# Turning the cross-attention's input on VectorE in 32x32 blocks instead of on TensorE

## What is computed

```python
x = _layernorm(x + attn(x, w_qkv, w_out))              # mixing: fft of q, k, v, cumulative sum of k*v, inverse fft
x = _layernorm(x + xattn(x, ctx, mask, W_q, b_q, ...)) # cross-attention, 16 heads of 32, 77 keys per batch
x = _layernorm(x + ffn(x, int4(kernel), bias, a, b))   # one 512x512 matmul with a rank-16 addition
```

## Time and profile before

| | |
|---|---|
| median of three runs | 940.3 us |
| the profiled execution | 941.81 us |
| span in it, first to last instruction | 939.4 us |
| TensorE busy | 885.9 us, 94% |
| VectorE busy | 669.9 us, 71% |
| ScalarE busy | 369.5 us, 39% |
| GpSimd busy | 373.9 us, 40% |
| mean granted TensorE clock | 0.975 of full speed |
| one loop step of `attend` | 58.0 us |

### The profile page before, as it was taken

The page is one execution under the profiler, slowest core; times in us unless marked ns, Lnnn a source line. Parts: engine busy times, 40 slices in busy tenths (PEclk is TensorE's granted clock), DMA queues, the critical chain, the costliest instruction groups (busy, mean ns, idle before and its releaser), DMA issues.

```text
span 939.4 us, 14604 instructions
## 1 busy us (share of the span) xinstructions
PE 885.9 (94%) x4284; PEld 733.5 (78%) x4284; DVE 669.9 (71%) x1132; ACT 369.5 (39%) x1403; POOL 373.9 (40%) x338
## 2 busy tenths in 40 slices
PE   5798999999999999999689999999999999999887
PEld 4683887888888888888578887888888888888675
DVE  3364467666666657567667978889788897988957
ACT  4152221212121111111487556665556655566611
POOL 2000364434353443315337544345343454434523
PEclk9897999999999999999789999999999999999999
DMA  6971710322314020104513140321403213030021
GB/s 184 283 203 48 177 45 34 102 66 70 95 39 134 22 68 23 67 24 143 180 23 101 30 136 11 97 67 32 132 11 94 67 44 119 12 93 19 18 79 45
DMA packets 85962, 76.02 MB, mean 81 GB/s; under 512 B 39895, under 2 KB 58583, under 8 KB 85919
## 3 DMA queue, kind: packets, MB, share of 16 engines
q1 hardware_dynamic: 85919, 75.49, 27.3%
HBM read 52.60 MB, written 22.87 MB: 80 GB/s over the span
## 4 chain that ended last, share of the span: by engine, by line
PE 37%; DVE 6%; ACT 5%; issue 2%; DVEq 0%; POOLq 0%; POOL 0%; ACTq 0%
PE shared_ps L130 28%; ACT probs L1410 4%; PE shared_ps L1204 3%; PE score_ps L130 3%; DVE score_ps L1715 2%; PE shared_ps L1166 1%; PE shared_ps L1237 1%; DVE top_s L1720 1%; ACT xT_hi L1423 1%; DVE xT_lo L1681 1%; DVE xT_lo L1673 1%; ACT qT_hi L1398 1%; DVE x_and_res L1761 0%; DVE pT_lo L1700 0%; DVE y L1739 0%
## 5 line engine op out<-in xcount | busy, mean ns | idle before, releaser
L1410 ACT ACTIVATE probs<-score_ps,top_s 128x77 f32<-128x77 f32 x512 | 158.8, 356 | 37.9 <-DVE top_s L1720 37.9
L1410 ACT ACTIVATION_READ_ACCUMULATOR probs<-score_ps,top_s 128x1 f32 x512 | 122.3, 239 | 0.0
L1559 POOL TENSOR_TENSOR probs<-probs,per_total 128x616 f32<-128x616 f32 x64 | 82.2, 1300 | 63.9 <-DVE per_total L1727 63.8
L1552 POOL TENSOR_TENSOR rstd<-ve,half_power 128x1 f32<-128x1 f32 x64 | 41.7, 652 | 153.4 <-DVE ve L1750 153.3
L1715 DVE COPY_PREDICATED score_ps<-hidden,masked 128x616 f32<-128x616 int32 x64 | 68.3, 1068 | 10.8 <-PE score_ps L130 10.5
L100 POOL TENSOR_TENSOR xT_lo<-x_tok,xT_hi 128x512 fp32r<-128x512 f32 x28 | 38.0, 1360 | 88.0 <-ACT xT_hi L96 88.0
L729 ACT ACTIVATE qT_hi<-vals 128x512 fp32r<-128x512 f32 x32 | 19.3, 628 | 119.1 <-POOL vals L776 103.8
L776 POOL TENSOR_TENSOR vals<-qs_prod 128x512 f32<-128x512 f32 x32 | 40.9, 1291 | 62.7 <-DVE qs_prod L862 62.7
L1417 ACT ACTIVATE pT_hi<-shared_ps 128x512 fp32r<-128x512 f32 (+1 forms) x96 | 47.7, 541 | 41.9 <-PE shared_ps L1204 41.6
L722 ACT ACTIVATE v_sb<-v_ps 128x512 f32<-128x512 f32 x32 | 18.9, 594 | 106.8 <-PE v_ps L130 106.8
L761 POOL TENSOR_TENSOR mix_rstd<-mix_ve,half_power 128x1 f32<-128x1 f32 x32 | 21.9, 686 | 94.3 <-DVE mix_ve L881 94.3
(11 more groups left out here) (210 smaller groups left out, 2641.4 us busy)
## 6 DMA issues: line engine op xcount, KB each, us to landing
x_tok<-in_x SPq DMA_DIRECT2D x32, 256.0 KB, 4.6
x_res<-in_x SPq DMA_DIRECT2D x8, 1024.0 KB, 7.3
x_between<-mix_x SPq DMA_DIRECT2D x32, 256.0 KB, 2.0
x<-x_between SPq DMA_DIRECT2D x8, 1024.0 KB, 5.6
x_tok<-x_between SPq DMA_DIRECT2D x8, 1024.0 KB, 5.7
out<-y_out SPq DMA_DIRECT2D x32, 256.0 KB, 2.0
wqkv_sb<-in_w_qkv SPq DMA_DIRECT2D x16, 192.0 KB, 5.6
keys_split<-w_q_hi SPq DMA_DIRECT2D x8, 154.0 KB, 5.3
```

The costliest lines, as they stand in the source:

```text
L1410: nc.scalar.activation(probs[:, t % 2, j * KEYS:(j + 1) * KEYS], score_ps[:, g, k * KEYS:(k + 1) * KEYS], ACT.Exp, bias=top[:, t % 2, j:j ...
L1552: nc.gpsimd.tensor_tensor(rstd[:, n:n + 1], ve[:, n:n + 1], half_power[:], ALU.pow).then_inc(rstd_ready, 1)
L1559: nc.gpsimd.tensor_tensor(p, p, per_total[:, t % 2, h * heads:(h + 1) * heads].unsqueeze(2) .to_broadcast([P, heads, KEYS]), ALU.mult).the ...
```

## The change

x1 is no longer turned by TensorE. It is loaded in quarters, VectorE turns 32x32 blocks in place, ScalarE copies the high part, and the low part is made by GpSimd for column groups 0 and 1 and by VectorE for groups 2 and 3. Groups 0 and 1 get memory of their own (`x1T_first`), groups 2 and 3 stay in oT. The four uses X0 to X3 of the shared banks are gone. The one x1 load of 1 MB becomes four DMAs of 256 KB, the one load of W_q sixteen. Cut to its core:

```diff
+def load_quarters(sp, tile, src, loaded):
+    for q, part in enumerate(by_quarter(src)):
+        sp.dma_start(quarters(tile)[q * BLOCK:(q + 1) * BLOCK, :, :], part).then_inc(loaded, 16)
...
 # mix_tokens, SP
-            sp.dma_start(x1_next[:], w_q_dram.rearrange("(c p) n -> p c n", p=P)).then_inc(wq_loaded, 16)
+            for c in range(NC):
+                load_interleaved(sp, x1_next, w_q_dram, c, wq_loaded)
...
-            sp.dma_start(x1_next[:], x1_dram[0].rearrange("(t p) d -> p t d", p=P)).then_inc(x1_loaded, 16)
+            load_quarters(sp, x1_next, x1_dram[0], x1_loaded)
...
 # mix_tokens, TensorE, between the two halves of the last projection
-                    for c in range(NC):
-                        for t in range(NT):
-                            last = nc.tensor.transpose(next_banks[c][:, t * P:(t + 1) * P],
-                                                       x1_next[:, t, c * P:(c + 1) * P], ident[:])
-                        last.then_inc(hand.filled, 1)
...
 # mix_tokens, VectorE, at the end
+            dve.wait_ge(x1_loaded, 16 * NC)
+            for c in range(NC):
+                turn_block_column(nc, x1_next, c, hand.x1_turned)
             for c in range(NC):
                 dve.wait_ge(hand.x1T_hi, c + 1)
-                nc.vector.tensor_tensor(x1T[1][:, c, :], next_banks[c][:], x1T[0][:, c, :].bitcast(F32),
-                                        ALU.subtract).then_inc(hand.freed, 1)
+                low_of_column(nc.vector, *column(x1T, c), x1_next, c, hand.x1T_lo[c // 2], 2)
...
 # attend, bank order
-              "O3", "X0", "X1", "X2", "F1", "X3", "T2", "P12", "Q0", "F2", "P20", "P21", "Q1", "T3", "Q2",
+              "O3", "F1", "T2", "P12", "Q0", "F2", "P20", "P21", "Q1", "T3", "Q2",
...
 # attend
-        x1T = oT
+        x1T_first = pair("x1T_first", [P, NC // 2, S])
+        x1T = [[(first if c < NC // 2 else o)[:, c, :] for c in range(NC)] for first, o in zip(x1T_first, oT)]
...
 # attend, TensorE, step
-                turn_x1(i + 1, s, 0)
-                turn_x1(i + 1, s, 1)
-                turn_x1(i + 1, s, 2)
                 project_f(i, s, 1)
-                turn_x1(i + 1, s, 3)
...
 # attend, ScalarE, step
                 split_probs(i, s, 0, 2)
+                split_x1(i + 1, s, 0)
+                split_x1(i + 1, s, 1)
                 split_probs(i, s, 1, 0)
...
                 exponentials(i, 2, 0)
-                split_x1(i + 1, s, 0)
-                split_x1(i + 1, s, 1)
                 split_x1(i + 1, s, 2)
                 exponentials(i, 2, 1)
                 split_x1(i + 1, s, 3)
...
 # attend, GpSimd, step
                 root(i, s, "O2")
+                split_x1(i + 1, s, 0)
                 bias_x2(i, s, 2)
                 root(i, s, "F0")
+                split_x1(i + 1, s, 1)
                 root(i, s, "O3")
                 bias_x2(i, s, 3)
...
 # attend, VectorE, step
                 split_probs(i, s, 0, 0)
+                turn_x1(i + 1, 0)
                 add_o(i, s, 1)
...
                 split_probs(i, s, 0, 1)
+                turn_x1(i + 1, 1)
                 invert_totals(i, 1)
...
                 measure(i, s, "O2")
+                turn_x1(i + 1, 2)
                 split_probs(i, s, 0, 2)
+                turn_x1(i + 1, 3)
                 softmax_top(i, 2, 0)
...
                 softmax_top(i, 2, 1)
-                split_x1(i + 1, s, 0)
                 measure(i, s, "O3")
-                split_x1(i + 1, s, 1)
                 split_x1(i + 1, s, 2)
                 normalize_o(i, s, 3)
                 add_f(i, s, 1)
                 invert_totals(i, 2)
                 split_x1(i + 1, s, 3)
```

More of the change, by code:

```diff
@@ L508, in __init__ @@
         self.filled, self.freed = sem("shared_filled"), sem("shared_freed")
-        self.x1T_hi, self.q_hi = sem("x1T_hi_ready"), sem("q_hi_ready")
+        self.x1_turned, self.x1T_hi = sem("x1_turned"), sem("x1T_hi_ready")
+        self.x1T_lo = [sem(f"x1T_lo_ready{n}") for n in range(2)]
+        self.q_hi = sem("q_hi_ready")
 def load_keys(sp, k_dram, hand, i):
@@ L747, in _ @@
             for c in range(NC):
+                act.wait_ge(hand.x1_turned, c + 1)
+                high_of_column(nc, x1T[0][:, c, :], x1_next, c, hand.x1T_hi)
+            for c in range(NC):
                 act.wait_ge(hand.filled, c + 1)
-                nc.scalar.activation(x1T[0][:, c, :], next_banks[c][:], ACT.Copy).then_inc(hand.x1T_hi, 1)
-            for c in range(NC):
-                act.wait_ge(hand.filled, NC + c + 1)
                 nc.scalar.activation(qT[0][:, c, :], next_banks[c][:], ACT.Identity,
@@ L1068, in norm_count, with after_projection @@
             return nth(i - 1, 2 * NT, s.norms.index(use))
+        def after_projection(eng, s):
+            if "O3" in s.order:
+                eng.wait_ge(filled, s.filled("O3"))
         def x2T_of(i, t):
@@ L1088, in load_x1 @@
                 wait_reuse(sp, x1T_hi, i * NC)
-                sp.dma_start(x1[:], x1_dram[i].rearrange("(t p) d -> p t d", p=P)).then_inc(x1_loaded, 16)
+                for lo in x1T_lo:
+                    wait_reuse(sp, lo, i * NC)
+                load_quarters(sp, x1, x1_dram[i], x1_loaded)
             def load_residual(i, s, reuse):
@@ L1159, in _ @@
         def _(pe):
-            def turn_x1(i, s, c):
-                if c == 0:
-                    pe.wait_ge(x1_loaded, nth(i, 1, 0) * 16)
-                use = f"X{c}"
-                wait_reuse(pe, freed, s.reusable(use))
-                for t in range(NT):
-                    last = nc.tensor.transpose(shared_ps[s.bank(use)][:, t * P:(t + 1) * P],
-                                               x1[:, t, c * P:(c + 1) * P], ident[:])
-                last.then_inc(filled, 1)
             def project_q(i, s, c):
@@ L1173, in project_q @@
                     pe.wait_ge(x1T_hi, nth(i, NC, NC - 1))
-                    pe.wait_ge(freed, s.emptied("X3"))
+                    for lo in x1T_lo:
+                        pe.wait_ge(lo, nth(i, NC, NC - 1))
                 wait_reuse(pe, freed, s.reusable(use))
-                pieces = [([w[:, k, c * P:(c + 1) * P] for w in w_q], [x[:, k, :] for x in x1T]) for k in range(NC)]
+                pieces = [([w[:, k, c * P:(c + 1) * P] for w in w_q], [x[k] for x in x1T]) for k in range(NC)]
                 split_matmuls(nc, shared_ps[s.bank(use)][:], pieces).then_inc(filled, 1)
@@ L1390, in split_x1 @@
             def split_x1(i, s, c):
[L1391 to L1393 removed]
+                act.wait_ge(x1_turned, nth(i, NC, c))
+                if c == NC // 2:
+                    after_projection(act, s)
+                high_of_column(nc, x1T[0][c], x1, c, x1T_hi)
             def split_q(i, s, c):
@@ L1853, in _ @@
             softmax_top(0, 2, 1)
+            for c in range(NC):
+                turn_x1(1, c)
             split_probs(0, s, 0, 0)
```

72 lines of the change are left out of this document (37 added, 35 removed).

## The result

The changed kernel takes 961.55 us (median of four runs: 958.96, 959.84, 963.25 and 965.04), the kernel before 940.62 beside it: 1.0223 times as long, 95% interval 1.0184 to 1.0261. Forecast were 955.7 us, and 946 to 964 as the range. The profiled execution took 958.96 us, where the sum in that frame gave 957.2: 1.8 us off.

A forecast was written before the change was run, and what follows sets the result against it. VectorE's gapless stretch from O0 to Q0 was taken as the bound. Six steps at 2.65 us, 15.9, less 0.5, on the profiled 941.81 gave 957.2, so 955.7 us for the median; range 946 to 964.

The forecast's parts named there:

- What bounds the step: Loop step of attend: VectorE works without a pause between O0 and Q0, 26.5 us, though TensorE is busier.
- F0 moves from 580.00 to about 581.25: Loop step: the first two VectorE turns stand uncovered ahead of split_x2(0), for which the feed-forward F0 waits.
- Blocking by the subtractions: GpSimd's new subtractions hold VectorE's mask and y_out in a loop step: maxima 3.1 us late, then 3.55.
- Q0 starts at 597.5 instead of 594.85: 2.65 us late: Loop step's end: late maxima, ScalarE's exponentials and high-part copy, then VectorE's subtraction delay Q0; the step grows as much.
- The two low parts that VectorE no longer makes don't help, since it waits for ScalarE there: Ahead of Q0: dropping two low parts of 0.6 to 0.65 us from VectorE saves nothing.
- The light case: Rival: GpSimd's subtractions block nothing, only the turns shift Q0, 1.45 us a step, 948.5 us; chance 0.18.
- TensorE loses 1.75 us: Loop step: 16 turns of x1 leave TensorE, 1.75 us by the trace, an estimated 4.4 by the skill page.
- TensorE stays the bound: Rival: VectorE's turns find gaps, each loop step drops by 1.75 us, 929.3 us; sign: split_x2(0) ends by 580; chance 0.11.
- The collision: Rival: GpSimd's bias_x2 holds VectorE's last low part ahead of Q0, 3.85 us a step, 962.9 us; chance 0.22.
- The end of the mixing and step 0: Outside the loop steps: TensorE loses 16 turns in each, VectorE gains four; gain of 0.25 us each, 0.5 together.
- Loads: Quartered x1 load lands ahead of the first turn, SP's slack covers W_q's 15 extra issues: no cost.
- Clock ... No loss: Loop step: TensorE busy for 55.3 of 60.7 us, 91%, keeps its full clock, so no time is lost.

The follow-up runs named there:

- Experiment 2: Kernel before, TensorE still turning x1, plus four VectorE turns of a spare tile at the change's places: 955.54 us, ratio 1.0155.
- experiment 3: Changed kernel with GpSimd's two subtractions started only after the masks of softmax_top(2,0) and softmax_top(2,1): 953.9 us, ratio 1.0150.
- experiment 5: Changed kernel, separate edits around the last low part: made earlier, 958.95 us; short or long memset ahead of it, 962.34 or 968.42; BN_STATS ahead of it, 976.26.
- the last version: Changed kernel with turns ahead of O0, earlier x1 load, group 3's low part earlier, GpSimd's second subtraction and normalize_probs(2,0) gated: 935.76 us, ratio 0.9931.
- experiment 4: Changed kernel with VectorE's four turns moved ahead of O0, x1 loaded half a step earlier: 950.95 us; with batch 2's x1 loaded in step 0: 944.27 us.

## Why the prediction was right, point by point

- **What bounds the step.** Right. TensorE at 57 of 58 us and VectorE at 49 looked like a bound by TensorE, but VectorE's list from O0 to Q0 waited for no other engine. (It was not quite "without a pause": five waits of 0.16 us for its own BN_STATS lie in it.) Experiment 2 shows it: work added on that list lengthens the step although nothing is taken from or given to TensorE.
- **"F0 moves from 580.00 to about 581.25".** 1.25 put down, 1.23 measured.
- **Blocking by the subtractions.** Maxima 3.1 us late put down, 2.91 measured; 3.55 behind y_out, measured 3.39. Both subtractions fell where they were put, and experiment 3 took 1.2 us a step back by moving them. The page "SBUF — State Buffer" of the Trainium skill, "Who interferes with whom", says that the instruction that starts first keeps the shared port for its whole length: this case's traces agree in both orders, 1.76 us for GpSimd behind VectorE in the changed kernel, 1.25 for VectorE behind GpSimd in experiment 5.
- **"Q0 starts at 597.5 instead of 594.85: 2.65 us late".** This term was undersized; 2.92 was measured and 3.05 for the whole step, 2.4 us in six steps (the profiled execution is only 1.8 off, because less of it lies outside the span). The step that failed is the one ahead of it: "The two low parts that VectorE no longer makes don't help, since it waits for ScalarE there". VectorE did not wait for ScalarE; the high part was ready at 659.97 and the low part started at 660.49, behind normalize_o(3), add_f(1) and the inverse of the totals. The chain to Q0 runs through VectorE's list (3.39 late at the maxima) and the two low parts saved 0.45 of it, not their 1.2: normalize_o(3) now waits 0.54 for a root that the low part of group 2 holds (1.07 us instead of 0.55). The chain by way of the exponentials, which gave 2.65, is the second one: in experiment 5 it releases Q0, 2.22 late. That a sum along it came so near was luck, since the two chains end within 0.7 us of each other.
- **The light case, 1.45 a step,** rested on the same wrong chain, and its sum leaves out the 0.25 us from the low part to Q0 that the forecast counts (1.7 with it). Without blocking it is 2.23 (experiment 2) or 1.8 (experiment 3, at full clock).
- **TensorE loses 1.75 us.** Its busy time fell from 57.05 to 55.83 us in a step at full clock, and to 55.54 in the last version: 1.2 to 1.5 us, near the 1.75 and far from the estimated 4.4.
- **TensorE stays the bound.** Right to leave out, but the sign named for it, F0 back by 580, does not decide it. In experiment 4 F0 is back and the step is still 58.18 us, because Q0 comes no earlier than in the kernel before: it waits for VectorE's last low part.
- **The collision.** Right as a mechanism. That VectorE came first, so that the sum could do without it, is luck: the prediction had it as a coin's toss.
- **The end of the mixing and step 0.** 0.5 us gained put down, 0.56 measured, but made of two parts that were not put down so: attend begins 1.4 us earlier (455.60 against 457.00), and 0.8 of it is gone again at the first O0.
- **Loads.** Nothing, as put down: no turn of x1 shows an idle mark for a DMA in the changed kernel. That this rests on the place of the turns is seen in experiment 4, where the same load cost 5.61 us.
- **"Clock ... No loss".** Wrong as to the clock, right as to the time. Behind the wait of 1.95 us the clock fell during F0, from full speed to 1.2 GHz. The window of a stretch in it, and O3 in a step where it did not fall:

```profile
647.00:648.00 1.00, 1.00 (x4) 0.73 (x3) 1.00 (x2) 0.00 (x0) 1.00 (x1) 0.50 0.05 7
```

```profile
772.60 0.50 PE L138 MATMUL shared_ps<-w_o_hi,xT_hi 128*128 128x512 f32 x1 [1.27 <-DVE y L1750]
```

F0 took 4.4 us instead of 2.8. But the step with 1.00 and the one with 0.97 are 61.12 and 61.11 us long: at full clock TensorE only waits 1.27 us at O3 for VectorE instead. (The prediction had put idle time ahead of F1; none is seen there.) The slack that made the change useless for TensorE also hid its slow clock.

What stays open is why executions of the changed kernel differ by up to 6 us. A low clock costs 0.6 us a step in F0 or 1.6 in Q0 in other kernels here, and a step in which GpSimd comes first at the last low part costs 1.2 or more. Either would be of that size, but the two executions of the changed kernel that have a trace, each the fastest of its series, show no such step.

## What to carry to other kernels

An engine that is 85% busy can still be the bound: look for the stretch in which its rows carry no idle mark for another engine, and put moved work outside it. Here the same four instructions cost some 16 us more in the gapless stretch than in VectorE's waits for ScalarE and ahead of a mask that was held anyway, provided that their load is issued early enough. Work given to GpSimd is not free for VectorE either: start it behind the mask or the normalization that it would hold, with a wait on that instruction.

## What the runs showed of the hardware

- GpSimd's addition bias_x2(3) took 1.28 us alone, 1.76 beside the low part, 1.90 with a memset of 0.17 us ahead of the low part and 2.30 with one of 0.48. With the longer memset between, its row began 0.47 to 0.54 us ahead of the low part's, and it was held in five steps and first in one; with BN_STATS between it began 0.51 to 0.57 ahead and was first in all six. So the lead alone does not decide, and a memset mostly keeps GpSimd out; why it did not in one step is not shown.
- VectorE's turns and BN_STATS ran beside GpSimd at their plain 0.70 and 0.68 us, while COPY_PREDICATED (1.55 us instead of 0.80), TENSOR_SCALAR from SBUF (1.02 instead of 0.54) and the subtraction of two SBUF operands (1.25 instead of 0.63) were held.
- The same wait of 1.95 us ahead of F0 was followed by a fall to 1.2 GHz in some loop steps and by full clock in others, in one and the same execution.
